# A two-layer language tower on one NeuronCore: weights and residuals folded into matmuls, index and softplus terms on GpSimd, and a new step order

## The reference, cut to what matters

```python
h = emb[x] + pos                                   # "token": two reversible layers
y1 = x1 + lsh_attention(layer_norm(x2, s, b)); y2 = x2 + ffn(layer_norm(y1, s, b)); h = (y1 + y2) / 2
# Mamba, once forward and once on the flipped sequence, on x = layernorm(h)
xi, z = split(x @ in_proj);  u = silu(conv(xi) + conv_b)
dt = softplus(dt_low @ dt_w + dt_b)                # dt_low, B, C = split(u @ x_proj)
state = exp(dt * A) * state + (dt * u) * B         # 16 states, sequential over 128 tokens
y = sum over states of state * C + u * Dskip;      out = (y * silu(z)) @ out_proj
x = ln(x + fwd + bwd, ln1_g, ln1_b)
h = h + ln(x + gelu(x @ w1 + b1) @ w2 + b2, ln2_g, ln2_b)
h = h + sum over experts of comb[e] * (gelu(x @ w1[e] + b1[e]) @ w2[e] + b2[e])     # x = layernorm(h)
h = h + attention(layernorm(h)); h = h + bitwise_network(layernorm(h))
```

## Time and profile before

| | before |
|---|---|
| median of 3 runs | 4150.01 us (4141.49 to 4173.7) |
| profiled execution | 4160.64 us |
| its span | 4158.5 us |
| DVE busy | 3647.5 us, 88% |
| PE busy | 3340.4 us, 80% |
| ACT busy | 3193.9 us, 77% |
| POOL busy | 1392.4 us, 33% |
| mean granted TensorE clock | 0.861 |

### The profile page before, as it was taken

How to read it: one execution, slowest core, us unless ns; L and a number is a source line. 1 busy time by engine, 2 the same in 40 slices (tenths; PEclk the granted TensorE clock), 3 DMA queues, 4 the chain that set the end, 5 groups by cost and what they waited for, 6 DMA issues and landing times.

```text
span 4158.5 us, 29909 instructions
## 1 busy us (share of the span) xinstructions
PE 3340.4 (80%) x8428; PEld 1457.7 (35%) x8428; DVE 3647.5 (88%) x3470; ACT 3193.9 (77%) x4047; POOL 1392.4 (33%) x612
## 2 busy tenths in 40 slices
PE   6564777879888888888888788888888788877687
PEld 4131423324343333434343333424333342423232
DVE  0599899998999999999999999999999999899942
ACT  2455888878788887978888897978888887786742
POOL 0334333243433333333333333343333333332300
PEclk7666788898888999988889998988989888798998
DMA  1233343433333343423343343333434343333410
GB/s 57 72 89 84 94 124 92 121 83 114 92 107 113 98 116 91 126 82 113 98 106 113 92 120 87 119 93 107 113 86 119 93 119 91 88 110 91 122 33 24
DMA packets 200822, 404.28 MB, mean 97 GB/s; under 512 B 17744, under 2 KB 26064, under 8 KB 200400
## 3 DMA queue, kind: packets, MB, share of 16 engines
q1 hardware_dynamic: 198608, 398.18, 33.5%
q0 software_dynamic: 2048, 4.20, 0.5%
HBM read 387.38 MB, written 14.94 MB: 97 GB/s over the span
## 4 chain that ended last, share of the span: by engine, by line
DVE 47%; PE 26%; ACT 18%; issue 8%; POOL 0%; DMA 0%; DVEq 0%; ACTq 0%; POOLq 0%; SPq 0%
DVE states L780 17%; DVE states L788 7%; ACT L575 6%; DVE y_sum L790 5%; PE bank_a L456 5%; PE bank_b L467 4%; ACT decay L575 3%; PE bank_p L394 3%; ACT L571 3%; ACT middle L575 2%; PE bank_q L404 2%; ACT tok L575 2%; PE bank_a L427 1%; DVE tok L806 1%; ACT last L575 1%
## 5 line engine op out<-in xcount | busy, mean ns | idle before, releaser
L1048 POOL TENSOR_TENSOR dbu<-dtu,bc_rows 128x1024 f32<-128x1024 f32 x512 | 1211.0, 2366 | 2319.9 <-DVE states L780 1168.6
L780 DVE TENSOR_TENSOR_SCAN states<-decay,dbu 128x1024 f32<-128x1024 f32 x512 | 1238.3, 2419 | 33.1 <-DVE decay L770 0.5
L575 ACT ACT_TABLE_LOAD x563 | 722.3, 1283 | 68.7 <-PE bank_a L427 37.4
L456 PE MATMUL bank_a<-middle,experts 128*128 128x512 f32 x1024 | 638.2, 709 | 165.3 <-ACT middle L575 156.8
L575 ACT ACTIVATE decay<-dt,neg_a 128x508 f32<-128x508 f32 x1024 | 674.4, 708 | 61.6 <-DVE states L780 53.7
L467 PE MATMUL bank_b<-middle,experts 128*128 128x512 f32 x1024 | 608.3, 680 | 37.6 <-ACT comb_t L575 24.7
L571 ACT ACT_TABLE_LOAD x394 | 505.5, 1283 | 162.2 <-DVE states L780 101.9
L575 ACT ACTIVATE middle<-bank_a,columns 128x512 f32<-128x512 f32 x576 | 396.0, 687 | 294.8 <-PE bank_a L456 219.2
L788 DVE TENSOR_TENSOR states<-states,bc_rows 128x1024 f32<-128x1024 f32 x480 | 591.3, 1232 | 15.2
L790 DVE TENSOR_TENSOR y_sum<-y_sum,states 128x1024 f32<-128x1024 f32 x480 | 585.8, 1220 | 16.3
L456 PEld LDWEIGHTS bank_a<-middle,experts 128*128 128x128 f32 x1024 | 190.0, 213 | 429.7 <-ACT middle L575 272.5
(11 more groups left out here) (208 smaller groups left out, 4480.3 us busy)
## 6 DMA issues: line engine op xcount, KB each, us to landing
bc_rows<-bc_scratch SPq DMA_DIRECT2D x512, 512.0 KB, 4.7
experts<-ew SPq DMA_DIRECT2D x128, 512.0 KB, 3.8
comb_rows<-comb_scratch SPq DMA_DIRECT2D x128, 256.0 KB, 3.8
h_scratch<-tok SPq DMA_DIRECT2D x16, 256.0 KB, 2.0
x_scratch<-xin SPq DMA_DIRECT2D x16, 256.0 KB, 2.0
xr<-x_scratch SPq DMA_DIRECT2D x16, 256.0 KB, 4.2
h<-h_scratch SPq DMA_DIRECT2D x16, 256.0 KB, 4.3
out<-last SPq DMA_DIRECT2D x16, 256.0 KB, 4.0
```

Of the source, the lines that this page charges most:

```text
L456: tick(mm(A, EW[:, e % 2, 128 * c:128 * c + 128], s_xn, start=True, stop=True), "e_h")
L575: return nc.scalar.activation(out, in_, func, **more)
L780: link(dve, nc.vector.tensor_tensor_scan(flat(hs), flat(da[:, n % AHEAD]), flat(dbu[:, n % AHEAD]), 0.0, ALU.mult, ALU.add), "a_scan")
L1048: tick(nc.gpsimd.tensor_tensor(dbu[:, n % AHEAD], dtu[:, k % 2], b, ALU.mult), "a_dbu")
```

## The change

It touches five things. First, arithmetic: norm weights of the middle are folded into the following weights or into constants (`scaled1`, `scaled2`, `mc1`, `mc2`, and `mw1` and its biases at the start); the residual x is added by a `centre` matmul that accumulates in the same bank as the output projection; `out_proj` and `mw2` are centred once at the start (`fold`), so that their product needs no `centre` matmul. The three sums at the end of `token` become two. The two halves of `gate`, of |x| and of `dt` become single instructions of 1024 columns, for which P and Q are now one tensor of two banks (the profile calls both `bank_p`).

Second, the softplus series is a square plus a constant, times e; POOL adds the constant and multiplies, and DVE needs one minimum instead of a minimum and a maximum. Third, the ids are turned into rows on POOL, ahead of the gather. Fourth, in the last layer q and k are computed by blocks of 128 features for all four sequences, and 16 matmuls with a selector of 2 columns (`heads`) sum the heads; the DVE reductions go. Some copies move from DVE to ACT (`t_va`, `t_y2`, `f_raw`). Fifth, `ORDER` is a new set of strings for all five engines.

Over the whole program DVE has 3188 instructions in place of 3476, ACT 3854 in place of 4049, of which 778 table loads in place of 957, PE 4744 matmuls in place of 4466 (each fp32 matmul is two records in the profile), and POOL 96 more.

```diff
 ORDER = {
     "ACT": (
-        "PACDPPPPPPPPPPPPPPPPPPPPPPPPPPPPPPPPPPPPPPPAAAPPPPPAPPAPAAPPAPPAPAPAPPAPPAPPPAAPAPAPPAPPAPAPAPPAPAP"
+        "PCPPDPAPPPPPPPPPPPPPPPPPPPPPPPPPPPPPPPPPPPAAAPPPAPAPPAPAPPPPAPAPAPAPPPPPPAPPAAPAAPPAPPPAAPAPPPPPAPA"
...
+    row_sums = small[:, 56:56 + 2 * HALVES + NF]
...
-    P, Q, A, B, C, E = (ctx.enter_context(nc.psum_tensor(f"bank_{x}", [128, T], F32))[:, :] for x in "pqabce")
+    PQ = ctx.enter_context(nc.psum_tensor("bank_p", [128, HALVES, T], F32))
+    P, Q = PQ[:, 0], PQ[:, 1]
+    A, B, C, E = (ctx.enter_context(nc.psum_tensor(f"bank_{x}", [128, T], F32))[:, :] for x in "abce")
...
 # PE, middle
-                        last = mm(A, w("fb"[d] + "out", a=128 * h, n=128), x[:, h],
-                                  start=(d == h == 0), stop=(d == h == 1))
-                tick(last, "c_yo")
-                yield from ln("c_", q, xr[:, :], ("c_xr", 2 * g + 1), A, B, s_sq)
-                yield from ffn("cf_", g, x1, "mw1", "mw2", ("c_ln", q + 1), A, B, c_slots)
-                yield from ln("c_", q + 1, xr[:, :], ("c_xr", 2 * g + 2), A, B, s_sq)
-                yield from ln("c_", q + 2, h1[:, :], ("c_h1", g + 1), A, B, s_sq)
+                mm(A, w("centre"), xr[:, :], start=True, stop=False)
+                yield
+                pe.wait_ge(s["a_yg"], 2 * g + 2)
...
+                        last = mm(A, w("fb"[d] + "out", a=128 * h, n=128), x[:, h], start=False, stop=(d == h == 1))
+                tick(last, "c_xc")
+                yield from variance(0, g)
...
+                            mm(B, w("scaled1"), x1, start=True, stop=False)
...
+                mm(B, w("centre"), h1[:, :], start=True, stop=False)
+                tick(mm(B, w("scaled2"), x1, start=False, stop=True), "c_xc")
+                yield from variance(2, g)
 # PE, last_layer
+                for j in range(SEQS):
+                    for c in range(4):
+                        at = 8 * j + 2 * c
+                        last = mm(C[:, at:at + 2], prods[:, c, blk(j)], w("heads"), start=True, stop=True)
+                tick(last, "a_sc")
 # ACT, pre
-                for h in range(HALVES):
-                    yield
-                    act.wait_ge(s["p_xz"], 4 * k + 3 + h)
...
-                    tick(af(gate[:, d, h], (P, Q)[h], ACT.Silu), "p_gate")
+                yield
+                act.wait_ge(s["p_xz"], 4 * k + 4)
...
+                tick(af(gate[:, d], PQ[:, :, :], ACT.Silu), "p_gate")
...
+                link(act, af(e_sp, PQ[:, :, :], ACT.Abs), "p_abs")
                 link(act, af(e_sp, e_sp, ACT.Exp, scale=-1.0), "p_ex")
-                tick(af(d_sp, e_sp, ACT.Identity, scale=-0.5, bias=col("one")), "p_lo")
-                tick(af(l_sp, e_sp, ACT.Ln, bias=col("one")), "p_l1")
+                tick(af(d_sp, e_sp, ACT.Square, scale=3 ** -0.5, bias=col("series")), "p_lo")
+                tick(af(l_sp, e_sp, ACT.Ln, bias=col("over1")), "p_l1")
 # DVE, pre
                 dve.wait_ge(s["p_l1"], k + 1)
-                link(dve, tt(l_sp, l_sp, e_sp, ALU.min), "p_k")
-                yield
                 dve.wait_ge(s["p_low"], k + 1)
-                link(dve, tt(l_sp, l_sp, d_sp, ALU.max), "p_k")
-                for h in range(HALVES):
-                    yield
-                    last = stt(dt[:, d, h], (Q, P)[h], 0.0, l_sp[:, h], ALU.max, ALU.add)
-                link(dve, last, "p_dt")
+                link(dve, tt(l_sp, l_sp, d_sp, ALU.min), "p_k")
+                yield
+                link(dve, stt(dt[:, d], PQ[:, :, :], 0.0, l_sp, ALU.max, ALU.add), "p_dt")
 # DVE, middle
-                dve.wait_ge(s["c_yo"], g + 1)
-                dve.wait_ge(s["c_ldx"], 16 * g + 16)
-                link(dve, tt(xr[:, :], A, xr[:, :], ALU.add), "c_xr")
-                yield from ln("c_", q, A, s_sq, x1, "mg1", "mn1")
-                yield
-                dve.wait_ge(s["cf_y"], NF * g + NF)
-                link(dve, stt(xr[:, :], B, col("mb2"), x1, ALU.add, ALU.add), "c_xr")
-                yield from ln("c_", q + 1, A, s_sq, x1, "mg2", "mn2")
+                yield from ln("c_", q, A, s_sq, x1)
+                yield from ln("c_", q + 1, B, s_sq, x1, "mc1")
...
-                link(dve, tt(h1[:, :], x1, h1[:, :], ALU.add), "c_h1")
-                yield from ln("c_", q + 2, A, s_sq, s_xn)
+                dve.wait_ge(s["c_xc"], 3 * g + 3)
+                tick(stt(h1[:, :], x1, col("mg2"), h1[:, :], ALU.mult, ALU.add), "c_h1")
+                yield from ln("c_", q + 2, B, s_sq, s_xn, "mc2")
 # DVE, token
-                link(dve, stt(y2, Q, col("tb21"), y2, ALU.add, ALU.add), "t_y2")
-                yield
-                link(dve, tt(y2, y1, y2, ALU.add), "t_y2")
-                yield
-                tick(ts(h_next, y2, 0.5, None, ALU.mult), "t_out")
+                tick(stt(h_next, y2, 0.5, Q, ALU.mult, ALU.add), "t_out")
 # POOL
                 pool.wait_ge(s["p_lo"], 2 * g + d + 1)
+                link(pool, nc.gpsimd.tensor_scalar(d_sp, d_sp, SERIES, None, ALU.add), "p_cubic")
                 tick(nc.gpsimd.tensor_tensor(d_sp, d_sp, e_sp, ALU.mult), "p_low")
```

353 lines of the change are left out of this document (210 added, 143 removed).

## The result

The changed kernel took 4089.13 us (median of 4 runs, 4083.86 to 4093.4) beside 4145.75 us of the kernel before in the same series. The ratio is 0.9845 with a 95% interval of 0.9804 to 0.9885: 1.5% faster, by something between 1.2% and 2.0%. The forecast was 3965 us. The sign was right and the time lies in the range, but the gain is about a third of what the sum said (57 us between the medians; the sum had 181). The profiled executions lie further apart, 4158.5 against 4086.7 us, which is 72 us, because the one of the kernel before is longer than its median; what follows accounts for these 72.

A forecast was written before the change was run, and what follows sets the result against it. DVE was taken to bound the steady groups. Terms 174 + 38 + 9 − 15 − 35 + 10 gave 181 us off 4158.5, 3969 scaled to the runs' median, called 3965 us with some waits going; range 3860 to 4105.

The forecast's parts named there:

- A microsecond taken off DVE shortens a group by nearly a microsecond: Steady groups: DVE, busy 225.6 of 239.1 us, sets the period until PE, at 202, or a wait holds it.
- 174 us of work: DVE: of net 251 us taken off it, the part that is work and not standing behind POOL, counted as gain.
- The term of the holding (38 of 77 us stay a gain): DVE at L806, L760 and L823: 77 us stood behind POOL's SBUF work; half, 38 us, was taken as gain.
- The end of 77 for the return: DVE beside POOL's dbu: at worst all 77 us of holding return, if two-input instructions take the freed places.
- POOL's addition, taken at 1.2 us with 2.37 as upper bound: POOL's 32 added one-input additions: 38 us, of which 4 in 10 meet DVE, costing 15 us.
- The change of direction (35 us): Softplus for the backward scan, after step 256: DVE's minimum stalls 2.3 us at 15 groups, ends 0 and 120.
- The second rival: Stall of 6 us a group at the minimum and all 77 us of holding returned: about 4062 us, chance 0.16.
- The fourth rival: Slower: the minimum behind step 256 waits longer than DVE saves, 13.5 us a group; 4200 to 4260 us, chance 0.05.
- What costs nothing: PE's narrow matmuls, 5.4 us a group, lie beside DVE; ACT stays covered; folding weights in the head costs 0.
- The signs that I named: Wrong if DVE's waits pass 15 us a group or busy time 218; recurrence above 2.5 us means holding returned.
- One sum of a rival: First rival, faster still: waits fall from 7.2 to 4 us a group, counted as 45 us; 3860 us, chance 0.12.
- The tail (10 us): Tail of 205.8 us: shorter middle norms and the residual's dropped step gain 10 us, ends 0 and 20.

The follow-up runs named there:

- e12: The kernel before, with eight of the 30 additions into y_sum a group on 64 columns in place of 1024: 4101.47 us, ratio 0.9863.
- e1: The changed kernel, with the softplus constant added by ACT and not by POOL, which keeps the product: 4074.9 us, ratio 0.9791 to the kernel before.
- e5: The kernel of e1, with POOL's ids and gather moved ahead of the softplus product: 4199.99 us, ratio 1.0109 to the kernel before.
- e2: The changed kernel, with the three instructions turning ids into rows back on DVE, the gather staying on POOL: 4138.47 us, ratio 0.9942 to the kernel before.
- e9: The kernel of e5, with the ids in two buffers and loaded one group earlier by SP: 4049.14 us, ratio 0.9729 to the kernel before.
- e7: The kernel of e1, with half of the second expert matmuls on 64 of 512 columns: 4074.19 us, ratio 0.9791 to the kernel before.

## Why the prediction was wrong in size

**"A microsecond taken off DVE shortens a group by nearly a microsecond": this step failed.** The waits (7.2 us a group) looked small, and I took the rest for work. e12 shows the worth on the kernel before: 3.2 us for 8. The whole change fits that. DVE's busy time without the holding counted above falls by 133 + 107 − 77 = 163 us, about 10 a group, and a group is 5.0 shorter. The forecast's 174 us of work was nearly right; its worth was half. What took the rest stands in the same profile: 30 us more holding (the next step) and 61 us more time in which DVE is not busy, 163 − 30 − 61 = 72. The forecast had 16 for the latter. e1 shows the exchange between the two, 4.3 us a group less busy and 3.9 more waiting. Why the waits grow, by which chain of PE or ACT, is not shown.

**The term of the holding (38 of 77 us stay a gain) had the wrong sign.** The 77 went, 107 came: 30 lost in place of 38 won (of the 107 the forecast had 15, as POOL's addition). The end of 77 for the return was no bound, since I held fixed how often DVE meets POOL. e12 and the rows near 1550 us show why it isn't: shorter work between two recurrences, or POOL behind by a gather, brings recurrences onto `dbu`. The rows to see it in were there: a `dbu` of 2366 ns behind each recurrence, and about 2.45 us of DVE work to cover it.

**POOL's addition, taken at 1.2 us with 2.37 as upper bound, is 3.1 us.** The bound was wrong: I took a product with two inputs as above anything with one. What I said of its effect, 15 us in all, is near the 16 us that e1's profile shows, but by another way: I had it in port time in every group, and e1 shows it until group 3, where POOL feeds the minimum late, and almost nothing after.

**The change of direction (35 us) was too dark, and in the wrong place.** The minimum waits 41.5 us in all, 22.2 of it once in the head, 14.1 until group 3, and 5.2 once in eleven steady groups. Before, L806 and L809 waited 21.5 in all, nothing of it in the steady groups. So the wait grew by 20 us, 15 of them before the steady part, where the forecast had 2.3 us at each of 15 groups. The second rival's stall did not come. The fourth rival's mechanism is real, as e5 shows, but the order keeps clear of it.

**"What costs nothing"** named the wrong cover for the ids: I gave their wait (29 us) as holding that goes, and never asked what ids and gather do to the third `dbu` behind them on POOL. The third recurrence takes 3.9 us more than the usual 2.3 and waits another 1.2 for its `dbu`, both in the mean of a group. In sum the move still pays, as e2 shows with 4.5 us a group.

**Right**: 778 table loads, ACT at 188.9 us a group (192 forecast), 197 instructions a group. PE was forecast at 3430 us and is 3347: the 512 narrow records take 65.9 us as estimated (67). q and k run at 659 and 653 ns where they ran at 732 and 689, 14 us less, but v at 875 where it ran at 604, 35 us more. So where the 83 us went was not found.

**The signs that I named** for a failure came for DVE's busy time, 219.2 us a group (over 218), and for the recurrence, 2.52 us in the mean (above 2.5, which was to mean that the holding came back there). The waits stayed below 15 us a group. The addition is over 2.4 us, so its term should have been more than doubled; the period is 234.1 us (226 to 230 forecast) and the tail 207 (190 to 200). One sum of a rival is off, without weight for the forecast: 3.2 us of waits less make 51 us in 16 groups, not 45.

**The tail (10 us) was half right.** From the last recurrence to the last expert matmul it is 119.8 us in place of 130.4, by the shorter norms. But what follows is longer. PE in the tail of the changed kernel:

```profile
4019.37 3.70 PE L543 MATMUL bank_c<-weights,last 128*128 128x2 f32 x32 [0.93 <-DVE last L1038]
4022.94 1.60 PE L549 MATMUL bank_e<-weights,last 128*128 128x512 f32 x2
4025.23 2.07 PE L549 MATMUL bank_e<-weights,last 128*128 128x512 f32 x2 [0.69 <-ACT last L635]
4027.99 2.07 PE L549 MATMUL bank_e<-weights,last 128*128 128x512 f32 x2 [0.69 <-ACT last L635]
4030.75 2.07 PE L549 MATMUL bank_e<-weights,last 128*128 128x512 f32 x2 [0.69 <-ACT last L635]
```

Before, v was computed between the q and k of the sequences. Now it comes behind the head sums, four times through bank E alone, the last three each behind ACT's copy: 13.2 us from 4019.4 to 4032.6 that lie in the open. From the last expert matmul to the end it is 87.3 us, where it was 75.4. No run has v on two banks or in its old place, so this reading is argued from the trace only.

The version that beats both kernels is e9: 4049.14 us, 0.9729 of the kernel before, with an interval that ends (0.9779) below where that of the changed kernel begins (0.9804). It leaves nothing of the computation out.

## What to carry to other kernels

An engine that is 94% busy need not be the bound if it shares a port, because time in which it is held counts as busy. Before a gain on it is counted one for one, take a known amount of its work away and read the period; here 8 us gave 3. Check as well that the cut took what it should: half of the second expert matmuls on an eighth of their columns gave 12 us a group and not 19. When the other engine answers each step with an instruction on that port, the work between the steps is its cover, and making it shorter gives little (here 0.4 for one in the kernel before). A move onto a lightly loaded engine is priced by what stands behind it in that engine's order (here the third product of a group), not by its share of busy time.

## What the runs showed of the hardware

- On POOL a one-input addition of a constant over 1024 fp32 columns took 2.77 us at the least and 3.1 in the mean; a two-input product of the same width took 2.38. The Trainium skill (GPSIMD Engine Reference, section 4.1 "Engine selection") has two-input operations on GpSimd about twice as slow as on VectorE and one-input ones near line rate. The first agrees (DVE takes 1.23 us for such a product, L854); by the second the addition should have been the shorter of POOL's two, and it is the longer.
- Instructions of four columns on DVE took 1.84 and 1.87 us in the mean (L939, L940 in e2) beside POOL's products, and 0.17 at the least.
- With less work for PE (e7) the granted clock of the steady part went from 0.89 to 0.86, the first expert matmuls became 6% longer (713 to 757 ns) and the uncut ones of the second 3% (686 to 704), so that 12 us a group taken away made PE's busy time 6.5 us shorter.
- A fp32 matmul record of 64 columns took 301 ns in the mean where one of 512 took 704 (e7), and one of 2 columns 264 ns (L543 of the changed kernel): an eighth of the columns was not an eighth of the time.
- Three `dbu` back to back held one recurrence for 4.26 us (6.56 in place of 2.30), at the same step in ten of eleven groups: DVE did not get the port between two of POOL's instructions.
